# A two-layer graph network on one core: dst loaded in two halves, x split partly by GpSimd, the target term made earlier

## The reference

```python
def _mp_layer(x, src, dst, edge_attr, W, b):
    src2, dst2 = concat([src, loops]), concat([dst, loops])
    ea2 = concat([edge_attr, zeros])
    msg = concat([x[dst2], x[src2], ea2], axis=1) @ W + b
    return relu(segment_sum(msg, dst2, num_segments=n))

h   = _mp_layer(x, src, dst, edge_attr, W1, b1)      # 64 -> 128
out = _mp_layer(h, src, dst, edge_attr, W2, b2)      # 128 -> 64
x   = layernorm(x + log_softmax(out))
```

## Time and profile before

| | us |
|---|---|
| median of 3 executions | 209.03 (208.85 to 209.24) |
| the profiled execution | 208.97 |
| its span, first to last instruction | 207.2 |
| busy PE / DVE / ACT / POOL in the span | 177.4 / 173.8 / 118.8 / 48.9 |
| granted TensorE clock, mean | 0.994 |

### The profile page before, as it was taken

One profiled execution on the slowest core, in us unless ns is written; L12 is line 12 of the kernel. 1 busy time (PEld: TensorE's weight loads), 2 busy tenths in 40 slices (PEclk: granted clock), 3 DMA queues, 4 the chain that ended last, 5 costly groups with the idle time before them and its releaser, 6 DMA issues.

```text
span 207.2 us, 5086 instructions
## 1 busy us (share of the span) xinstructions
PE 177.4 (86%) x2019; PEld 162.7 (79%) x2019; DVE 173.8 (84%) x495; ACT 118.8 (57%) x234; POOL 48.9 (24%) x56
## 2 busy tenths in 40 slices
PE   0515399999999999999899999999996999999950
PEld 0104299888988989889779889798996999999940
DVE  0889999999999999999999989921019999999873
ACT  2336649778997997888889989984220201111101
POOL 8388998305000692003004000000000000000000
PEclk9999999999999999999999999999999999999997
DMA  1334101000000000000000000000000010011010
GB/s 41 106 93 116 24 4 36 0 4 2 3 0 4 0 5 0 3 1 3 0 4 0 5 0 3 2 3 0 3 0 0 3 30 10 3 40 25 22 22 20
DMA packets 8886, 3.32 MB, mean 16 GB/s; under 512 B 8146, under 2 KB 8411, under 8 KB 8861
## 3 DMA queue, kind: packets, MB, share of 16 engines
q1 hardware_dynamic: 8061, 2.04, 4.8%
q0 software_dynamic: 800, 0.93, 1.9%
HBM read 2.15 MB, written 0.81 MB: 14 GB/s over the span
## 4 chain that ended last, share of the span: by engine, by line
PE 61%; DVE 29%; issue 3%; ACT 3%; DMA 2%; DVEq 0%; ACTq 0%
PE pset L1016 17%; PE acc L975 15%; PE pset L961 13%; DVE ohr L514 8%; DVE ohl L514 7%; PE acc L1016 7%; PE epb L1002 3%; PE epb L1010 2%; DMA adj<-in_dst 2%; PE epb L990 2%; DVE adj L504 2%; ACT adj L816 1%; DVE adj L463 1%; PE epb L1003 1%; PE epb L992 1%
## 5 line engine op out<-in xcount | busy, mean ns | idle before, releaser
L816 ACT ACTIVATE adj<-pset 125x1000 bf16<-125x1000 f32 (+7 forms) x100 | 81.1, 836 | 15.1 <-PE pset L961 12.0
L975 PE MATMUL acc<-x,adj 125*125 125x195 bf16 x625 | 67.8, 252 | 0.0
L961 PE MATMUL pset<-ohr,ohl 128*125 128x125 bf16 x625 | 54.4, 232 | 8.7 <-DVE ohr L514 8.1
L961 PEld LDWEIGHTS pset<-ohr,ohl 128*125 128x125 bf16 x625 | 47.7, 146 | 13.8 <-issue 6.6
L975 PEld LDWEIGHTS acc<-x,adj 125*125 125x125 bf16 x625 | 57.1, 139 | 0.3
L514 DVE TENSOR_TENSOR ohl<-iota,keys 128x1000 bf16<-128x1000 bf16 (+1 forms) x79 | 52.5, 664 | 0.7 <-ACT keys L799 0.5
L514 DVE TENSOR_TENSOR ohr<-iota,keys 128x1000 bf16<-128x1000 bf16 (+1 forms) x79 | 52.5, 664 | 0.0
L1016 PE MATMUL pset<-z,adj 125*125 125x192 bf16 x425 | 37.0, 247 | 1.8 <-DVE x L661 1.8
L1016 PEld LDWEIGHTS pset<-z,adj 125*125 125x125 bf16 x425 | 35.5, 136 | 2.4 <-DVE x L661 2.0
L903 ACT ACTIVATE x<-x 125x192 f32<-125x192 f32 (+2 forms) x6 | 2.6, 427 | 34.5 <-DVE x L670 34.5
L384 POOL CAST stats<-se 125x15 bf16<-125x15 f32 x5 | 5.4, 1071 | 54.3 <-DMA se<-se_scratch 54.3
(11 more groups left out here) (120 smaller groups left out, 169.3 us busy)
## 6 DMA issues: line engine op xcount, KB each, us to landing
x_nat<-in_x_tiles SPq DMA_DIRECT2D x1, 406.2 KB
x_nat<-in_x_tiles SPq DMA_DIRECT2D x1, 375.0 KB
out<-x SPq DMA_DIRECT2D x2, 187.5 KB
out<-x SPq DMA_DIRECT2D x3, 93.8 KB
adj<-in_dst SPq DMA_DIRECT2D x1, 208.5 KB
out<-x SPq DMA_DIRECT2D x1, 125.0 KB
adj<-in_edges,adj POOLq DMA_INDIRECT x5, 4.3
adj<-in_edge_attr,adj POOLq DMA_INDIRECT x5, 3.5
```

Of the source, the lines that this page charges most:

```text
L816: ins = act.activation(adj4[0:Q, g, :, i * WD:(i + n) * WD].rearrange("p h (w e) -> p h w e", e=WD), rows[:, w - k * SET:w - k * SET + n, ...
L961: ins = pe.matmul(pset[k % 2][0:Q, i // 4, i % 4 * 128:i % 4 * 128 + WD * G], ohl[k % 3][:, i // 2, :, i % 2], ohr[k % 3][:, i // 2, :, i ...
L975: ins = pe.matmul(acc[g % 2][0:Q, 0:XW], adj4[0:Q, g, h, :], x3[:, h, :], start=(h == 0), stop=(h == G - 1))
```

## The change

1. `dst` is loaded by two DMAs, rows 0 to 62 (`QA` = 63) from SyncE's queue and rows 63 to 124 from ScalarE's, each with its own semaphore. SyncE and VectorE wait for both.
2. The cast of `dst` to fp16 moves from VectorE to ScalarE.
3. The two subtractions for x's first part (groups 0 to 11) move from VectorE to GpSimd: the first between `gather_attrs(0)` and `gather_edges(1)`, the second between `gather_edges(1)` and `gather_attrs(1)`. ScalarE's middle cast of that part moves ahead of its copies of the keys. Each part has semaphores of its own, and layer 1 starts when part one is split; it waits for part two at block 12 of group 0.
4. `base_of` for groups 0 to 11 and 12 to 15 moves to the place after the last layer-1 reduction; 16 to 24 stays after the first batch. `f_t`, its scratch, lies in the end of `x3`.
5. In a batch the operations per group become one subtraction over the batch, placed behind the square of y, and one multiplication at the end.

```diff
+QA = 63
 # gpsimd
             gather_edges(0)
             gather_attrs(0)
+            gp.wait_ge(xs_ready, 1)
+            gp.tensor_tensor(x_rest[:, 0:XA, :], x_nat[:, 0:XA, :], x3[:, 0:XA, 0:C], ALU.subtract).then_inc(xa_rest, 1)
             gather_edges(1)
+            gp.wait_ge(xa_mid, 1)
+            gp.tensor_tensor(x3[:, 0:XA, 2 * XC:2 * XC + C], x_rest[:, 0:XA, :], x3[:, 0:XA, XC:XC + C], ALU.subtract)\
+              .then_inc(xa_low, 1)
             gather_attrs(1)
 # vector
-            dve.wait_ge(dst_in, 16)
-            dve.tensor_scalar(rows16[:, 0:EC], dst_rows[:, 2:EC + 2], -float(MID), None, ALU.add).then_inc(rowsf_ready, 1)
+            for s in dst_in:
+                dve.wait_ge(s, 16)
...
             key_sums(0)
-            rest_of_x(0, 0, XA)
             dve.wait_ge(consts, 8)
             dve.wait_ge(keys_ready, 1)
             onehots(0)
             onehots(1)
             bias_rest(0)
-            low_of_x(0, 0, XA)
             onehots(2)
-            rest_of_x(1, XA, G)
+            rest_of_x()
             bias_rest(1)
             attr_sums(0, 0, WD)
             onehots(3)
-            low_of_x(1, XA, G)
+            low_of_x()
...
             reduce_sums(G - 1)
+            dve.wait_ge(b2_in, 16 * 2)
+            for j in range(J):
+                dve.wait_ge(se_in[j], 16)
+            base_of(0, BATCHES[1][1])
+            base_of(BATCHES[1][1], BATCHES[2][1])
             z_rest(last - 1)
...
-            dve.wait_ge(rest_ready, len(EPILOGUES))
-            base_of(0, BATCHES[1][1])
...
-                flink(dve.tensor_tensor(r, y, y, ALU.mult))
+                fpost(dve.tensor_tensor(r, y, y, ALU.mult))
+                dve.wait_ge(fch, fc[0] - 1)
+                flink(dve.tensor_tensor(o, p, c.unsqueeze(2).broadcast_to([Q, n, C]), ALU.subtract))
...
-                for k in range(n):
-                    ins = dve.tensor_scalar(f_v[i % 2][:, k, :], f_p[:, k, 0:C], f_c[:, k:k + 1], f_r[:, k:k + 1],
-                                            ALU.subtract, ALU.mult)
-                flink(ins)
+                flink(dve.tensor_tensor(vv, o, r.unsqueeze(2).broadcast_to([Q, n, C]), ALU.mult))
...
-                    base_of(BATCHES[1][1], G)
+                    base_of(BATCHES[2][1], G)
 # scalar
+            act.dma_start(dst_rows[QA:Q, :], dst[QA:Q, :]).then_inc(dst_in[1], 16)
             act.preload_act_table_set("natural_log_exp_and_others")
+            for s in dst_in:
+                act.wait_ge(s, 16)
+            act.activation(rows16[:, 0:EC], dst_rows[:, 2:EC + 2], ACT.Copy, bias=-float(MID)).then_inc(rowsf_ready, 1)
...
             cast_x(0, 0, XA)
+            cast_middle_x(0, XA, xa_rest, xa_mid)
...
             copy_keys(acc[0][:, 0:2 * Q], 0)
-            cast_middle_x(0, 0, XA)
 # tensor, layer1
-                        pe.wait_ge(xl_ready, 2)
+                        pe.wait_ge(xa_mid, 1)
+                        pe.wait_ge(xa_low, 1)
...
                 for h in range(h0, h1):
+                    if g == 0 and h == XA:
+                        pe.wait_ge(xb_mid, 1)
+                        pe.wait_ge(xb_low, 1)
 # sync
-            sp.dma_start(dst_rows, dst).then_inc(dst_in, 16)
-            sp.wait_ge(dst_in, 16)
+            sp.dma_start(dst_rows[0:QA, :], dst[0:QA, :]).then_inc(dst_in[0], 16)
+            for s in dst_in:
+                sp.wait_ge(s, 16)
```

More of the change, by code:

```diff
@@ L289, in gnn @@
         keys_ready = sem("keys_ready")
-        xs_rest = sem("xs_rest")
+        xa_rest = sem("xa_rest")
+        xa_mid = sem("xa_mid")
+        xa_low = sem("xa_low")
+        xb_rest = sem("xb_rest")
+        xb_mid = sem("xb_mid")
+        xb_low = sem("xb_low")
         xs_ready = sem("xs_ready")
-        xm_ready = sem("xm_ready")
-        xl_ready = sem("xl_ready")
         bmask_ready = sem("bmask_ready")
@@ L520, in onehots, with rest_of_x, low_of_x @@
                 ins.then_inc(oh_ready, 1)
[L522 to L531, removed]
+            def rest_of_x():
+                dve.wait_ge(xs_ready, 2)
+                dve.tensor_tensor(x_rest[:, XA:G, :], x_nat[:, XA:G, :], x3[:, XA:G, 0:C], ALU.subtract).then_inc(xb_rest, 1)
+            def low_of_x():
+                dve.wait_ge(xb_mid, 1)
+                dve.tensor_tensor(x3[:, XA:G, 2 * XC:2 * XC + C], x_rest[:, XA:G, :], x3[:, XA:G, XC:XC + C], ALU.subtract)\
+                   .then_inc(xb_low, 1)
             def bias_rest(k):
@@ L615, in _ @@
             z_low(last - 2)
[L616 to L621, removed]
             fc = [0]
@@ L646, in base_of @@
                 flink(dve.tensor_tensor(base[:, a:b, :], base[:, a:b, :], late_part, ALU.add))
+            reduce_sums(G - 1)
             dve.wait_ge(b2_in, 16 * 2)
@@ L650, in _ @@
                 dve.wait_ge(se_in[j], 16)
-            dve.wait_ge(rest_ready, len(EPILOGUES))
             base_of(0, BATCHES[1][1])
+            base_of(BATCHES[1][1], BATCHES[2][1])
+            z_rest(last - 1)
+            z_low(last - 1)
+            z_rest(last)
+            z_low(last)
+            dve.tensor_reduce(deg_sum[:, :], stats[:, :, 0], AX.X, ALU.add).then_inc(deg_ready, 1)
             na = 0
@@ L787, in cast_x, with cast_middle_x @@
                 act.activation(x3[:, a:b, 0:C], x_nat[:, a:b, :], ACT.Copy).then_inc(xs_ready, 1)
-            def cast_middle_x(i, a, b):
-                act.wait_ge(xs_rest, i + 1)
-                act.activation(x3[:, a:b, XC:XC + C], x_rest[:, a:b, :], ACT.Copy).then_inc(xm_ready, 1)
+            def cast_middle_x(a, b, rest, mid):
+                act.wait_ge(rest, 1)
+                act.activation(x3[:, a:b, XC:XC + C], x_rest[:, a:b, :], ACT.Copy).then_inc(mid, 1)
             cast_x(0, 0, XA)
+            cast_middle_x(0, XA, xa_rest, xa_mid)
             def copy_keys(bank, j):
@@ L868, in _ @@
             cast_bias(2)
-            cast_middle_x(1, XA, G)
+            cast_middle_x(XA, G, xb_rest, xb_mid)
             for k in range(2, LEAD):
```

2 lines of the change are left out of this document (1 added, 1 removed).

## The result

The changed kernel takes 210.68 us (median of 4, 210.65 to 210.71) against 209.03 before: 1.0078 times as long, 95% interval 1.0061 to 1.0096. Its profiled execution has a span of 208.9 us, 1.7 more than before. The direction and the range of the prediction held; the size was 1.65 in place of 0.77.

What follows compares the result with a forecast made beforehand. Bound: a serial start, layer 1 alternating between TensorE and VectorE, and layer 2's TensorE stream with one hole. Terms +0.90 - 0.49 - 0.09 + 1.25 + 1.25 - 1.97 - 0.12 = +0.73 gave 209.8 us, range 207.0 to 211.2.

Steps and rivals of the forecast that it cites:

- dst in two halves: Load at the start: 62 rows get only two engines, the fullest carries 38 packets for 25, +0.90 us.
- The cast on ScalarE: Start: VectorE's cast of dst goes and ScalarE's runs beside the first two picks, -0.49 us.
- The low part off VectorE: Ahead of one-hots 2: 0.87 us leaves VectorE, which then waits for ScalarE's cast; only -0.09 us remains.
- The two holds: Chain to the keys: each GpSimd subtraction holds up VectorE's two-input operations, +1.25 us each.
- the price of the subtraction: GpSimd's subtraction of 125x768: 1.3 us from twice its cast's slope, bounds 0.75 and 4.8.
- Layer 1: Builds and layer 1: the start's change carries through one for one; beginning on part one is worth nothing.
- Target term: Start of layer 2: moved into VectorE's idle stretch, it closes TensorE's hole near 158 us, -1.97 us.
- One multiplication: Last batch: three operations go, one subtraction and one multiplication replace them, -0.12 us.
- no hold: Rival at the keys: GpSimd's subtractions don't hold VectorE up; -1.77 us, 207.3, chance 0.22.
- one hold: Rival at the keys: only one subtraction holds VectorE up; -0.52 us, 208.5, chance 0.14.
- The halves coming no later: Rival at the dst load: two halves land no later; 208.9, down to 207.6 if spread widely, chance 0.08.
- The rival on TensorE's pace: Rival in layer 1's builds: the slow pace lasts some 3 sets longer; up to +2.7 us, 212.5, chance 0.09.

Runs made afterwards that it cites:

- first_on_gp: The changed kernel with only the first subtraction of x's part one on GpSimd, the low part on VectorE: 208.95 us, 1.0005 times the kernel before.
- x_on_dve: The changed kernel with both subtractions of x's first part back on VectorE, middle cast behind the key copies: 207.78 us, 0.9933 times the kernel before.
- dst_80_45: The changed kernel with dst split into 80 and 45 rows in place of 63 and 62: 208.78 us, 0.9988 times the kernel before.
- best_iota: The kernel best with GpSimd's iota of 256 elements moved behind gather 0: 207.83 us, 0.9945 times the kernel before.
- second_on_gp: The changed kernel with only the second subtraction on GpSimd, the first on VectorE, middle cast behind key copies: 208.10 us, 0.9963 times the kernel before.
- best: x_on_dve (changed kernel, x's first part split on VectorE) with dst in 80 and 45 rows: 205.57 us, 0.9845 times the kernel before.
- best_again: The kernel best, unchanged, measured once more beside best_iota_early on the same chip: 205.57 us, 0.9846 times the kernel before.

## Why the prediction was right, and where its sizes were off

The terms, in the prediction's order, each as forecast and as the two traces show it:

- *dst in two halves*, +0.90: VectorE's first step starts 1.02 later (5.71 for 4.69). Right in mechanism and, by the packet counts, in its number of engines.
- *The cast on ScalarE*, -0.49: the first pick product starts 0.56 later in all (6.71 for 6.15), so -0.46. ScalarE's cast of 0.56 us is hidden beside the picks, as said.
- *The low part off VectorE*, -0.09: from the one-hots to build 4 the loss goes from 3.95 to 3.84, so -0.11. VectorE waits 0.69 us for ScalarE's cast ahead of the second rest of x, as said.
- *The two holds*, +2.50: 1.41 and 1.98, 3.39 together. This is the term that was mis-sized, by 0.89. The step that failed first is the price of the subtraction: 1.60 us on GpSimd, where twice the slope of a cast gave 1.3; that is 0.6 for the two. The page "GPSIMD Engine Reference" of the Trainium skill (section "3.1 Elementwise — side-by-side cycle accounting", 4497 ns for 2048 elements) gave an estimated 1.7, nearer to the measured 1.60, and would have put the sum at 210.5. The second step that failed, worth the other 0.3, is the place of the second hold. The prediction had the second subtraction ahead of lines 494 and 496; in fact the rounding step just before (490 of the kernel before), left out because it has one input, was held by gather 1 from 14.89 to 15.40 and then by the subtraction to 17.05. Being caught by the gather first made it 1.98 and not about 1.6. The first hold didn't fall on the row named either: the first subtraction started at 12.25, not near 12.0 as worked out, because x's cast ended at 12.16, and it held the count of offset 4 (line 472). That cost little: where the named step was caught, in first_on_gp, it was 1.29 in place of 1.41.
- *Layer 1*, 0: +0.07 (3.84 at build 4, 3.91 at the last 33 matmuls).
- *Target term*, -1.97: -2.03 (3.91 to 1.88 at the end of the stream).
- *One multiplication*, -0.12: -0.18 from the last matmul to the end of the span (7.57 for 7.75). Of this 0.13 lies between the square and the last multiplication.

They sum to +1.70, the difference of the spans. So the direction came out for the stated reason, the mutual hold, which no row had shown beforehand; had the holds been absent, the same sum would have said 207.3. Of the rivals, no hold and one hold are out: x_on_dve and first_on_gp show both. The halves coming no later is out by the cast at 5.72.

The rival on TensorE's pace did not decide here, but it is where the 0.4 us of x_on_dve can hide. Eight matmuls of a build take 1.09 us up to some point and 0.65 after it; the granted clock reads 1.00 through both stretches, so no row tells which level holds. That point does not follow the work: it lies between 31.8 and 32.7 us in both kernels below, though the dense work starts 3.24 us apart. Both lists are from TensorE's timeline, first the changed kernel (from its first dense set at 29.60), then x_on_dve (from 26.36):

```profile
31.79 1.01 PE L971 MATMUL pset<-ohr,ohl 128*125 128x125 bf16 x8
32.64 0.85 PE L989 MATMUL acc<-x,adj 125*125 125x195 bf16 x8
33.33 0.64 PE L971 MATMUL pset<-ohr,ohl 128*125 128x125 bf16 x8
```

```profile
30.71 1.06 PE L971 MATMUL pset<-ohr,ohl 128*125 128x125 bf16 x8
31.57 1.27 PE L989 MATMUL acc<-x,adj 125*125 125x195 bf16 x8
32.68 0.65 PE L971 MATMUL pset<-ohr,ohl 128*125 128x125 bf16 x8
```

x_on_dve falls back from 0.60 behind the kernel before at the one-hots to 0.98 at the start of layer 1's last 33 matmuls. The other traces point the same way. Counted from the first dense set, three builds are slow in full (1.06 us or more) in x_on_dve, dst_80_45, best_iota and second_on_gp. From the first one-hots to the last 33 matmuls it is 123.93, 123.79 and 123.88 us in the first three (the fourth has its own hold in this stretch), and 123.36 to 123.69 in all nine kernels with fewer. So a third slow build goes with a loss of 0.1 to 0.6 us. One slow build fewer than in best gave nothing (best_again, 123.56 against 123.52). No kernel was built to change the pace alone, so that the slow builds cause it stays argued.

## What to carry to other kernels

Work moved to GpSimd isn't free for VectorE: look at what VectorE has queued beside each GpSimd operation, gathers and memsets included, and price the move by that operation's whole length if the step it meets is on the chain. Split a load so that each part's row count has a large divisor up to 16: 80 and 45 rows landed 2.2 us before 63 and 62, and 1.2 before all 125 in one load. Work that makes the chain wait late, here the target term, can go into an earlier idle stretch of its own engine: that gave the 2 us worked out for it.

## What the runs showed of the hardware

- A VectorE operation with two SBUF inputs waits for a GpSimd operation that reads: 0.66 became 2.08 us beside a subtraction of 1.60, and a step of 0.16 became 1.45. Beside a memset of 1.38 us it kept its 0.66.
- A one-input `tensor_scalar` waits for GpSimd writes too: 0.29 became 0.58 beside the memset, 0.25 became 0.69 beside an iota, and 0.29 became 0.54 beside the generation of a gather.
- A VectorE operation that waits doesn't always come next: with the following GpSimd operation 0.02 to 0.03 us behind, it waited out both, 2.44 and 2.25 us. How the first of these came to be held while only the gather ran is open.
- Not every `tensor_scalar` is held by a gather. In the changed kernel two of them (0.29 and 0.22 us, from int32 pairs, at 14.43 and 14.63) ran inside gather 1 (14.03 to 15.40) unharmed, and in best fp16 comparisons inside gather 0 kept 0.25. The rounding step (f32 to f32) was held to the gather's end or longer in all five traces in which it started 0.6 us or more into one, and took 0.25 to 0.29 where it started together with one or 0.03 us ahead of it (x_on_dve, best). What tells these forms apart was not tried.
- GpSimd subtracts 125x768 f32 in 1.60 us; VectorE takes 0.95 for the same step (line 571 of x_on_dve, at 14.57).
- By the closing packets a load of 62 rows used two engines of sixteen, of 63 nine, of 45 fifteen.
